# A two-layer perceiver block: late expert tiles selected on VectorE, rows loaded between weights, a retention with early transposes and a time mixing in split products

## The reference

```python
x = x + L0_xattn(layernorm(x), ctx, ctx, mask)   # 16 heads of 32, 2048 keys per batch
x = x + L0_attn(layernorm(x))                    # retention: 16 query heads, |q.k|^2 with decay
x = x + L0_ffn(layernorm(x))                     # router 512->2048->8, top 2 of 8 experts, 512->2048->512
x = x + L1_xattn(layernorm(x), ctx, ctx)         # the same, with a layernorm at its end
x = x + L1_attn(layernorm(x))                    # time mixing, below
x = x + L1_ffn(layernorm(x))                     # router 512->8, top 2 of 8 experts, gate/up/down 512x512
```

```python
xn = layernorm(x) * ln_w + ln_b; prev = rows of xn shifted down by one, zero first
xk, xv, xr = xn * tm + prev * (1 - tm)          # three mixes, tm = tmk, tmv, tmr
k, v, r = xk @ Wk.T, xv @ Wv.T, sigmoid(xr @ Wr.T)
S[t] = sigmoid(decay_w) * S[t-1] + k[t] * v[t]
out = x + r * (S @ Wo.T)
```

## Time and profile before

| | |
|---|---|
| median of 3 runs | 2386.46 us |
| the profiled execution | 2385.33 us, its span 2383.6 us |
| mean granted clock of TensorE | 0.95 of 2.4 GHz |
| busy: PE, DVE, ACT, POOL | 2137.9, 1397.9, 1343.4, 352.0 us |
| DMA | 262.58 MB, mean 110 GB/s |
| cross attention 1, retention | from 0 and from 698 us |
| experts 1, cross attention 2 | from 895 and from 1381 us |
| time mixing, experts 2 | from 2087 and from 2168 us |

### The profile page before, as it was taken

The page is one execution under the profiler, slowest core; times in us unless marked ns, Lnnn a source line. Parts: engine busy times, 40 slices in busy tenths (PEclk is TensorE's granted clock), DMA queues, the critical chain, the costliest instruction groups (busy, mean ns, idle before and its releaser), DMA issues. The chain is left out here.

```text
span 2383.6 us, 37629 instructions
## 1 busy us (share of the span) xinstructions
PE 2137.9 (90%) x14685; PEld 1627.4 (68%) x14685; DVE 1397.9 (59%) x2352; ACT 1343.4 (56%) x2571; POOL 352.0 (15%) x302
## 2 busy tenths in 40 slices
PE   6999999999967977699999879999999999666797
PEld 4777777787735546588888646887787877433575
DVE  4455455454536653499999744445454545464587
ACT  2566566565634423488888525665665656402574
POOL 3111112121110000300000121121121211102501
PEclk9999999999988988899999879999999999877899
DMA  4000001010021003799999530010101010013786
GB/s 150 19 32 24 28 28 37 19 37 19 1 96 79 1 1 126 287 355 361 360 362 357 178 137 19 19 36 19 37 19 36 19 37 1 1 71 124 304 338 235
DMA packets 53727, 262.58 MB, mean 110 GB/s; under 512 B 9512, under 2 KB 9896, under 8 KB 26672
## 3 DMA queue, kind: packets, MB, share of 16 engines
q1 hardware_dynamic: 47104, 244.71, 27.5%
q0 software_dynamic: 2560, 8.39, 1.1%
q10 hardware_dynamic: 3888, 7.08, 0.8%
HBM read 243.91 MB, written 16.25 MB: 109 GB/s over the span
## 5 line engine op out<-in xcount | busy, mean ns | idle before, releaser
L508 DVE COPY c_pt<-bank 128x512 f32<-128x512 f32 x256 | 177.1, 692 | 549.4 <-PE bank L342 549.3
L658 ACT ACTIVATE c_pr<-wide,c_nmax 128x512 f32<-128x512 f32 x512 | 349.3, 697 | 165.5 <-DVE c_nmax L500 84.0
L231 POOL TENSOR_TENSOR c_clo<-c_raw,c_chi 128x512 fp32r<-128x512 f32 x128 | 167.5, 1313 | 1008.0 <-ACT c_chi L635 1008.0
L342 PE MATMUL bank<-ident,c_pr 128*128 128x128 f32 x2048 | 268.2, 273 | 13.0 <-DVE c_pt L508 10.2
L342 PEld LDWEIGHTS bank<-ident,c_pr 128*128 128x128 f32 x2048 | 237.6, 140 | 49.2 <-DVE c_pt L508 12.4
L92 PE MATMUL bank<-c_wv_hi,c_chi 128*128 128x512 f32 x512 | 217.6, 425 | 20.0 <-POOL c_clo L231 18.6
L1656 DVE TENSOR_TENSOR moe_wlo<-moe_raw,moe_whi 128x2048 fp32r<-128x2048 f32 x97 | 219.2, 2286 | 19.7 <-ACT moe_whi L1516 19.6
L643 ACT ACTIVATE c_khi<-bank,c_cols 128x512 fp32r<-128x512 f32 x128 | 88.1, 688 | 252.3 <-PE bank L94 252.3
L92 PE MATMUL bank<-c_chi,c_wk_hi 128*128 128x512 f32 x512 | 213.7, 417 | 9.2 <-ACT c_v L649 9.1
L94 PE MATMUL bank<-c_wv_hi,c_clo 128*128 128x512 f32 x512 | 202.4, 395 | 0.0
L93 PE MATMUL bank<-c_wv_lo,c_chi 128*128 128x512 f32 x512 | 202.2, 395 | 0.0
(11 more groups left out here) (355 smaller groups left out, 4029.6 us busy)
## 6 DMA issues: line engine op xcount, KB each, us to landing
moe_hr<-in_L_ffn_w SPq DMA_DIRECT2D x68, 1024.0 KB, 6.9
moe_raw<-in_L_ffn_w SPq DMA_DIRECT2D x52, 1024.0 KB, 7.0
c_raw<-in_ctx SPq DMA_DIRECT2D x32, 1024.0 KB, 4.9
moe_raw<-in_L_ffn_we_gate SPq DMA_DIRECT2D x15, 1024.0 KB, 7.1
moe_raw<-in_L_ffn_we_up SPq DMA_DIRECT2D x15, 1024.0 KB, 5.8
moe_raw<-in_L_ffn_we_down SPq DMA_DIRECT2D x15, 1024.0 KB, 6.1
slot_outputs<-moe_ob ACTq DMA_DIRECT2D x27, 256.0 KB, 7.0
ret_w<-in_L_attn_w_attn SPq DMA_DIRECT2D x4, 1024.0 KB, 9.0
```

The costliest lines, as they stand in the source:

```text
L231: nc.gpsimd.tensor_tensor(clo[:, g % 2, c, :], raw[:, c, :], f32(chi[:, g % 2, c, :]), ALU.subtract) \
L342: last = pe.transpose(TB[n % 2][:, h * P:(h + 1) * P], pr[:, u % 2, h, n * P:(n + 1) * P], k["ident"][:])
L508: nc.vector.tensor_copy(pt[:, n, :], TB[0][:]).then_inc(pt_dve, 1)
L658: nc.scalar.activation(pr[:, u % 2, h, :], S[h][:], ACT.Exp, bias=nmax[:, b % 2, i, at:at + 1], scale=-1.0 if masked else 1.0, accum_out=d ...
```

## The change

Block 0 of the keys: piece 0 of `clo` stays on POOL, pieces 1 to 3 go to DVE behind the cut of `wv`. In the second cross attention ACT's `deviations()` stands ahead of `split_weights(wv)`.

```diff
-                for c in range(C):
-                    low_part(0, c)
+                low_part(0, 0)
+                def low_first():
+                    for c in range(1, C):
+                        dve.wait_ge(chi_done, c + 1)
+                        nc.vector.tensor_tensor(clo[:, 0, c, :], raw[:, c, :], f32(chi[:, 0, c, :]), ALU.subtract).then_inc(clo_done, 1)
...
                     cut_weights(wv_lo, wv_raw, wv_hi, wv_split, wv_cut)
+                    low_first()
-                split_weights(wv_hi, wv_raw, wv_in, wv_split)
                 if x_in is None:
                     deviations()
+                split_weights(wv_hi, wv_raw, wv_in, wv_split)
```

```diff
-        xn = m.sb("xn", [P, D])
-        xT = m.sb("xT", [P, C, P])
+        xn = m.sb("xn", [P, NB, D])
+        xT = m.sb("xT", [P, NB, C, P])
                 project(0)
+                for b in range(1, NB):
+                    turn_x(b)
                 turn_qk(0)
...
                 for b in range(NB):
-                    if b + 1 < NB:
-                        turn_x(b + 1)
                     scores(b)
```

```diff
-    LATE = 1 if first else 2
+    LATE = 2
...
                 sp.wait_ge(s_["scattered"], 16 * 2 * NB)
-                for i, (a, b) in enumerate(CHUNK):
-                    sp.dma_start(rows_in[:, a - 1:b - 1, :], xg[a * P:b * P, :].rearrange("(i p) d -> p i d", p=P)).then_inc(xg_in[i], 16)
-                sp.wait_ge(s_["owners"], 1)
...
+                load_rows(0)
                 for n in range(ahead, len(stream)):
+                    if n == ahead + 3:
+                        load_rows(1)
+                    if n == ahead + 9:
+                        sp.wait_ge(s_["late_turned"], LATE)
+                        load_rows(2)
+                    if n == ahead + 12:
+                        load_owners()
                     load(n)
...
+                weigh_pairs()
+                late_tiles()
+                if not first:
                     low(0, 0)
-                    low(1, 0)
                 low_x(0)
+                low(1, 0)
...
                 for b in range(NB):
+                    add_back(b)
                     dve.wait_ge(s_["y_made"], b + 1)
                     nc.vector.tensor_tensor(x[:, b, :], x[:, b, :], ps[b][:], ALU.add).then_inc(s_["out"], 1)
```

```diff
+                for i in range(KINDS):
+                    for c in range(C):
+                        if i == 0:
+                            nc.vector.tensor_tensor(rise[:, c], zT[:, c, :, 1:P + 1], zT[:, c, :, 0:P], ALU.subtract)
+                        mix(i, c)
+                        if c > 0:
+                            low(i, c - 1)
+                    low(i, C - 1)
+                    low_weights(i + 1)
...
+                for b in range(NB):
+                    for o in range(C):
+                        nc.vector.tensor_tensor_scan(state[:, o, b, :], rate[:, o, :], kv[:, o, b, :], 0.0, ALU.mult, ALU.add) \
+                            .then_inc(s_["state"], 1)
+                    dve.wait_ge(s_["shi"], b + 1)
+                    nc.vector.tensor_tensor(slo[:, :, b, :], state[:, :, b, :], f32(shi[:, :, b, :]), ALU.subtract) \
+                        .then_inc(s_["slo"], 1)
```

More of the change, by code:

```diff
@@ L998, in _ @@
                     keep_projection(0, g)
+                for b in range(1, NB):
+                    keep_xT(b)
                 gates(0)
@@ L1475, in _ @@
                 place_first()
+                for l in range(LATE):
+                    turn_late(l)
                 if first:
@@ L1823, in stage_rwkv @@
 def stage_rwkv(nc, k, t, x, x_out):
+    KINDS = 3
     with ExitStack() as ctx:
@@ L1969, in _ @@
                     dve.wait_ge(s_["r"], b + 1)
[L1970 to L1972 removed]
+                    s.then(nc.vector.tensor_tensor(r[:, b, :], r[:, b, :], ps[b][:], ALU.mult))
                     nc.vector.tensor_tensor(x[:, b, :], x[:, b, :], r[:, b, :], ALU.add).then_inc(s_["done"], 1)
```

323 lines of the change are left out of this document (167 added, 156 removed).

## The result

The changed kernel takes 2319.08 us (median of 4 runs, 2317.28 to 2321.53) against 2386.72 (2384.07 to 2389.07) of the kernel before: ratio 0.9718, 95% interval 0.9701 to 0.9734. A second series of five runs gave 2322.37 and 0.9728 (0.9714 to 0.9741). The forecast was 2314, between 2300 and 2332. The profiled execution took 2317.28, its span is 2315.5, 68.1 less than before.

The account below looks back on a forecast made before the run. PE, busy nine tenths, was taken to bound the stages' long middle parts, so only the seams could win; the terms sum to 72.5 us, taking the profiled 2385.33 to 2312.8 and the median to 2314, range 2300 to 2332.

Parts of the forecast that it names:

- first keys: Start of the first cross attention: PE's first product comes earlier with three low parts on DVE; 4.0 us, bounds 0 and 4.6.
- second cross attention: Its start: square root ahead of ACT's cast, low parts on DVE, PE starts earlier; 4.8 us won, bounds 2 and 6.5.
- retention: Second batch: PE's wait for normalised rows and the half clock behind it go; 12.0 us won, bounds 7.5 and 14.
- router of the first experts: Router's first split moved ahead of the rows' splits, a swap of work PE needs both; 0, bounds 1.5 either way.
- first experts, start: Start of the tiles: weights no longer queue behind 3.7 MB of rows; 8.5 us won, bounds 2 and 10.
- first experts, end: Last tile's copy no longer waits behind sums, and PE's join runs at full clock; 11.0 us won, 0 at half clock.
- time mixing: Split products replace float32 products and DVE sets the end; 19.7 us won, bounds 22 and a loss of 20.
- second experts: stall, rows, scatter: Second experts: stall of 14.3 us goes, rows' DMA between weights costs 4.5, slower scatter issues cost 1.0.
- second experts, end: Three of four second sums and three of four last sums move ahead of the last gather; 3.7 us won.
- rival 1: Rows and owners between weights empty both rings: first experts' start wins 2, second experts pay 8.3; 2327 us, chance 0.18.
- The stall of 14.3: Second experts, around the late tiles: the 14.3 us stall, with POOL needing 31.0 for sixteen selections, was to go.
- three signs of being wrong: ACT waiting over 8 us for weight DMAs in either experts' stage, half clock beyond time mixing's first 5, scatter over 16.

Follow-up runs that it names:

- Rows at once: Changed kernel with the rows of both experts loaded in one go ahead of the weights, owners' reads behind them; 2324.93 us, ratio 0.9745.
- rows by tile: Changed kernel with the rows of the second experts in twelve loads (2 tiles, 2 tiles, then single tiles) instead of three; 2314.97 us, ratio 0.9712.

## Why the prediction was right, and where it was off

By its steps, against the first profile of the changed kernel:

| step | said | measured |
|---|---|---|
| first keys | 4.0 | 2.9 |
| second cross attention | 4.8 | 6.6 |
| retention | 12.0 | 10.4 |
| router of the first experts | 0 | 1.9, of it 1.5 the clock's chance |
| first experts, start | 8.5 | 7.5 |
| first experts, end | 11.0 | 11.1 |
| time mixing | 19.7 | 18.1 |
| second experts: stall, rows, scatter | 8.8 | 6.3 |
| second experts, end | 3.7 | 3.6 |
| sum | 72.5 | 68.1, with 0.3 lost between these places |

- **Reading the seams was right.** PE's waits, and the half clock behind them, hold about 50 of the 68; the other 18 are the time mixing, where the products became cheaper as well (45.6 instead of 56.6 from first to last). Retention, the end of the first experts and the start of the tiles came out within 1.6. Of the 7.5 at the start of the first experts' tiles the order of the transfers accounts for 5.7; the other 1.8 were not isolated. That the clock comes back with the wait was the step with the widest bounds (0 to 11 at the end of the first experts); the run with the old order of the sums shows it.
- **Some 5 of the 68.1 are not steady.** The first profile has the earlier full clock in the router (1.5) and at the end of the first experts (1.6), and 2.0 at the end of the second cross attention, which some other profiles of the same code lack; no step of the prediction had them. The medians won 67.6 and 64.1, so the 72.5 was 5 to 8 too high, and the errors of single places below are no more exact than these differences.
- **First keys, 1.1 less.** PE's first product came 4.2 earlier, not 4.6: VectorE's three low parts take 2.96 beside POOL's piece, and the forecast gave them 2.1. Behind it 1.3 are given back, which was not traced; the stage takes 697.7 to 700.0 in four profiles with the old code and 693.9 to 696.6 in ten with the new.
- **Retention, 1.6 less than said.** The numerators of the second batch come 11.5 earlier and those of the last 11.9. From the last numerators on 1.5 are given back, most of it at the lower clock: their products take 4.3 instead of 3.7, the last transposes 2.0 instead of 1.0, the last 16 products 9.0 instead of 8.8.
- **Second cross attention, 1.8 more.** PE's first product came 4.6 earlier, near what was said (4.8). PE reached the full clock sooner behind it, but that was lost again to 3.4 us of half clock later; the other 2.0 come from the last 37 us of the stage, where the granted clock is 0.86 and not 0.81. This gain is not steady: from the statistics in its middle to its end the stage takes 433.0 to 433.2 in the four profiles with the old code, 430.9 to 431.4 in six of the nine with the root ahead, and 433.0 to 434.5 in the other three. The forecast was right for its own place, and what came on top was in no step of it.
- **Time mixing, 1.6 less.** The last sum was to end 61.1 behind the stage's start and ends at 62.2; another 0.5 is lost between that sum and the next stage (1.4, before 0.9). Left out were VectorE's three waits of 1.12 for ACT's high part of the next weight block, where the forecast had said that it has no gaps; other terms of its sum were too large by 2. With these waits gone and the second rows moved forward the stage is 1.6 to 1.9 shorter, and PE and VectorE end it level. Which part of the 18.1 is the split products', which the single pass of statistics' and which the work by batches', no run separates.
- **Second experts: the rows between the weights were mis-sized**, 8.3 in one place and not 4.5. The prediction set DMA's free time over the whole stage against the rows; but the ring of four has no lead to spend, so 2 MB in one piece are paid at once and free time that comes later is lost. Rows at once are cheaper by 2.4, rows by tile by 3.7; by tile the loss is 4.6, near the 4.5 of the forecast, so its share of free time was right and the lump was its error. Here rival 1 was right with its 8.3; its other half, a start of the first experts that wins only 2, was not (7.5 measured, with 8.5 said).
- **The scatter got faster**, 12.1 from first issue to last end instead of 13.2, because sixteen selections of 0.27 now stand where 2048-column low parts stood. The forecast had charged 1.0 here and won 1.1. Of the rule of the Trainium skill (SBUF — State Buffer, Who interferes with whom) the first half is borne out by the copy (an issue of 2.11), with the multiplication not told apart from it; that a `tensor_tensor` was not seen to stall an issue is contradicted by 2.75 here.
- **The stall of 14.3 was no constant.** It was 14.3 in the kernel before, 12.7 and 13.0 with only the retention or the cross attentions new, and 5.5 in the profiled execution with only the time mixing new: POOL has three long pairs and about 31 in the first three of these traces, two pairs and 24.2 in the last. It was a term of the sum that depended on where VectorE's low parts fell beside POOL's selections and on how long the tile before had waited.
- **Its own signs were mixed.** Right were PE's first products (14.4, and 14.3 behind the stage's start), 1.0 of idle PE before the scores, and clock 1.0 in the join. Missed were transposes never over 7 apart in the first experts (8.0), VectorE without gaps in the time mixing, and no gap over 10 but a small one in the second experts (17.8). Of the three signs of being wrong two came: ACT waits 18.1 in the second experts for weight DMAs (over 8; in the kernel before it was already 14.3), and the clock is 0.50 until 16.8 us into the time mixing, beyond its first 5. The time was right all the same: in the second experts PE lost 8.3 in one tile and little elsewhere, and in the time mixing it has products in only 3.8 of the 16.8 us.

## What to carry to other kernels

Look at the seams: a short wait of TensorE can cost several times its length in products at half clock, so moving a copy of 0.7 ahead of sums of 6.3 was worth 7 to 8 here. Before loads are put between weights, count all DMA of a period, stores too, against the ring's lead: here a piece of 2 MB in a ring of four was paid in full, pieces of 256 KB cost about what didn't fit. And profile the same kernel twice before a difference of 3 us in a stage is given a cause, and look where the profiled execution lies among its runs: one of them was 4.9 below its median.

## What was not expected of the hardware

- With the same code and the same start, full clock came 2.9 apart in two executions, and a stage was 3.1 longer; the other stages agree within 0.5, except the last (205.1 and 210.1).
- Sixteen selections on GpSimd took 31.0 or 24.2 with the same code: 0.79 each, but 2.5 to 5.0 beside VectorE's subtractions of 2048 columns, of which more or fewer lay beside them.
- An indirect DMA's issue on GpSimd takes 0.97. One that begins inside a long instruction of VectorE outlasts it: 2.75 beside a subtraction, 2.11 beside a multiplication with a copy behind it; beside selections of 128 columns it takes 1.00, and 0.97 when the long instruction begins 0.70 into it.
